# A graph layer and a recurrence on one core: states kept by step, the edge places found earlier, the first norm reordered

## The chip, the cores and the metric

One core of a Trainium2 chip. The metric is the device time of one execution in microseconds.

## The reference

```
x = x + gnn(layernorm(x))     # h = z W + b; mean over incoming edges of h[src], by dst; dst is sorted
x = x + ffn(layernorm(x))     # a recurrence over the 3125 rows, hidden state h, cell c, 256 wide each
step: i = sigmoid(xi + h V_i); g = tanh(xg + h V_c); o = sigmoid(xo + h V_o)
      c = h * c + i * g;  h = o * tanh(c)
```

x is 3125 x 256, f32, with 103,125 edges. The recurrence runs once over all rows in order; its batch is 1.

## The kernel before

**Recurrence.** The 3125 rows are cut into 125 chunks of 25 steps, which run side by side from zero, and the chunks are run again from the end of the chunk before until starts and ends agree; t counts these steps, from 1 to DONE = 70. Steps 1 to HIDDEN = 20 run inside the counting loop (`early_*`). Steps 21 to ROUGH = 28 use one product of f16 parts, later ones three. The last round is t = 46 to 70 (`LAST_ROUND` = 45). Each step is done in two halves q of 63 and 62 chunks. On DVE a half is `new_part` (L1551, ig), `cell` (L1557, c_st), and `state_next`, which waits for ACT's tanh (L863) and writes h as f16 (h16) and then as f32 in `h_states` (L1562). POOL makes the f16 rest of h (`low_part`, L618) and h times c (`old_part`, L623). PE multiplies (`full_products`, L1103): 24 products, then a wait for the rest, then 8 for the gates i and g and 4 for o. ACT has the gates (L849, L857) and the seeds of the next step in PSUM (L836, L842).

**Layout.** `h_states` lies in h_flat as (group of five steps, half of H, chunk, step in the group), so one step's columns lie five apart. Block j of 125 rows (5 chunks of 25 rows) has its x in `x_sb[:, j, :]`.

**Output.** From t = 51 on, each step ends with one block turned on PE (two transposes, `turn_out`, L1144) and added to x on DVE (`add_out`, L1614, 256 columns), after both halves; five more blocks follow at t = 70. SP stores them in six pieces of five DMAs each (L505), waits for all (L511), and then comes to `where_far` (L464), which every engine runs: it waits for a flag, loads it, and skips a general path. DVE finds that flag from the gap between starts and ends (L1653 to L1665).

**Start.** SP loads dst and the 25 parts of x (L486 to L490), ACT's queue loads w_gnn and its bias, then U, V and b of three gates (L692 to L700). DVE takes moments of the first two chunks of five blocks, then the largest and smallest of w_gnn (L1296), then scales, the deviation of chunk 0 (L1278), the low part of W, the split bias and `window_starts` (L1349), the search for the first edge of each window; POOL gathers rows (L561) and edges (L574) for it. Then the loop over blocks (L1370): ACT normalizes (L713) and rounds (L735, L740), PE transposes (L964) and multiplies (L975, L978), DVE makes the low parts (L1387, L1393), takes the moments of block j + 10 and, in the first three blocks of a chunk, the deviation of the next.

**Edges.** After that loop PE turns the window edges (L985), DVE works out from src and dst the places and keys of 625 windows of 128 edges (L1404 to L1428, with `places`, L1248), and the counting loop (L1513) begins: one-hots on DVE (L1485), counts (L1061) and sums (L989, L991) on PE, with the second norm, gates and early steps in it. PE waits for keys and for all lines before it (L1049, L1050). Two tables hand-place the rest: `weights_work` (L1470) puts the halving of the weights at window (0, 15), four reductions of U and V at (1, 0) to (2, 0), and so on. POOL's `weights_top` (L566) reduces over partitions, and `root` (L581) does the inverse roots of the second norm.

## Time and profile before

| | us |
|---|---|
| median of 3 runs | 576.62 (575.88 to 580.61) |
| profiled execution | 576.53 |
| its span, first to last instruction | 574.7 |
| outside the span | 1.83 |
| PE, DVE, ACT, POOL busy | 433.1, 406.2, 361.0, 216.2 |

A row of instructions gives the start in us from the span's start, the duration, engine and line, what is written and read, how many were merged, and in brackets the idle time before and what ended it. "PEld" is PE's weight load, "SPq" the queue on which SP issues DMAs, "issue" is time in which the engine waited for nothing that the profile shows. bank and ps tiles lie in PSUM; early tiles all carry the name gx, because they lie in it.

### The profile page before, as it was taken

Reading aid. Unit: us, or ns where it says so; the run is one execution under the profiler, and the core shown is the slowest. Engines: PE = TensorE matmul, PEld = TensorE weight load, DVE = VectorE, ACT = ScalarE, POOL = GpSimd, SP = SyncE. Lnnn points to the kernel's source line nnn. Section 1 sums busy time; section 2 is a strip of 40 time slices with the busy share of each in tenths; the row PEclk is TensorE's granted clock in tenths of the full one; section 3 lists DMA queues with packets and bytes.
Section 4 is the critical chain, followed back from the end, with each engine's and each line's share of the span. In section 5 each row is a group of like instructions: output and inputs, shape, how many; then the busy total and the mean of one; then the engine's idle time right before and its main releaser. Section 6 shows DMA issues by size and latency. Waiting matters only on the chain.

```text
span 574.7 us, 15746 instructions
## 1 busy us (share of the span) xinstructions
PE 433.1 (75%) x6225; PEld 375.2 (65%) x6225; DVE 406.2 (71%) x1124; ACT 361.0 (63%) x961; POOL 216.2 (38%) x407
## 2 busy tenths in 40 slices
PE   1008891787999899999999998754877777777760
PEld 1006670575788788888888896644766667666660
DVE  0195769978777686877788784457677777777772
ACT  0024670454556677776867775688788888777750
POOL 5104000016243253443453543312556555555530
PEclk9999996699999999999999999975899999999995
DMA  7432003300010000001000100100000000011102
GB/s 179 146 120 50 2 1 97 104 25 2 1 47 1 1 26 22 2 1 46 2 2 13 35 2 1 46 1 1 3 3 3 5 2 2 10 41 47 43 12 89
DMA packets 17319, 17.79 MB, mean 31 GB/s; under 512 B 2294, under 2 KB 16889, under 8 KB 17239
## 3 DMA queue, kind: packets, MB, share of 16 engines
q1 hardware_dynamic: 12935, 13.03, 7.0%
q10 hardware_dynamic: 2864, 1.97, 1.5%
...
q14 instruction: 28, 0.23, 0.1%
...
## 4 chain that ended last, share of the span: by engine, by line
PE 40%; DVE 32%; ACT 12%; issue 6%; SPq 3%; POOL 3%; DMA 1%; DVEq 0%; ACTq 0%
PE bank L1020 9%; PE bank L989 8%; PE bank L991 8%; DVE c_st L1557 7%; DVE ig L1551 5%; ACT tc L863 5%; DVE h L1562 5%; PE bank L978 4%; PE bank L1061 4%; SPq L490 3%; DVE h_flat L1562 3%; DVE hots L1485 3%; ACT gx L754 2%; PE bank L1103 2%; PE bank L1037 2%
## 5 line engine op out<-in xcount | busy, mean ns | idle before, releaser
L989 PE MATMUL bank<-h_flat,counts 125*128 125x257 f16 x625 | 170.9, 275 | 0.0
L991 PE MATMUL bank<-h_flat,counts 125*128 125x256 f16 x625 | 169.0, 272 | 0.0
L1103 PE MATMUL bank<-h,V 128*128 128x63 f16 (+1 forms) x3216 | 123.3, 196 | 48.2 <-DVE h L1562 45.0
L797 ACT ACTIVATE counts<-bank 125x500 f16<-125x500 f32 (+1 forms) x175 | 97.3, 557 | 95.7 <-PE bank L1061 94.2
L1103 PEld LDWEIGHTS bank<-h,V 128*128 128x128 f16 x3216 | 110.5, 99 | 62.4 <-issue 43.3
L1061 PE MATMUL bank<-hots 128*128 128x125 f16 x625 | 136.7, 226 | 17.7 <-DVE hots L1485 17.6
L1485 DVE TENSOR_TENSOR hots<-iota,kp 128x1024 f16<-128x1024 f16 x157 | 105.1, 698 | 0.1
L593 POOL TENSOR_SCALAR newton<-rstd,var_eps 125x1 f32<-125x1 f32 x50 | 42.5, 850 | 122.6 <-DVE rstd L1445 113.4
L1061 PEld LDWEIGHTS bank<-hots 128*128 128x128 f16 x625 | 60.4, 99 | 29.4 <-DVE far_f L1428 12.5
L618 POOL TENSOR_TENSOR h<-h_flat,h 128x126 f16<-128x126 f32 x82 | 42.0, 512 | 66.6 <-DVE h_flat L1562 66.6
L1020 PE MATMUL bank<-z2T,U 128*128 128x250 f16 (+1 forms) x540 | 58.5, 260 | 10.7 <-DVE z2T L1457 6.0
L989 PEld LDWEIGHTS bank<-h_flat,counts 125*128 125x128 f16 x625 | 61.7, 99 | 7.3
L991 PEld LDWEIGHTS bank<-h_flat,counts 125*128 125x128 f16 x625 | 61.6, 99 | 0.7
L1020 PEld LDWEIGHTS bank<-z2T,U 128*128 128x128 f16 x540 | 45.3, 100 | 20.1 <-issue 9.2
L1562 DVE SCALAR_TENSOR_TENSOR h<-gate,tc 128x126 f16<-128x126 f32 (+1 forms) x100 | 30.0, 300 | 31.4 <-ACT tc L863 31.1
L849 ACT ACTIVATE gate<-bank,w_unscale 128x252 f32<-128x252 f32 x100 | 46.6, 467 | 6.5 <-PE bank L1103 5.4
L863 ACT ACTIVATE tc<-c_st 128x126 f32<-128x126 f32 x100 | 30.9, 309 | 28.1 <-DVE c_st L1557 28.1
L1557 DVE SCALAR_TENSOR_TENSOR c_st<-hc,ig 128x126 f32<-128x126 f32 x100 | 44.9, 449 | 3.4
L754 ACT ACTIVATE gx<-bank,gb,gx_scale 128x250 f32<-128x250 f32 (+1 forms) x90 | 42.3, 524 | 6.1 <-PE bank L1020 6.0
L623 POOL TENSOR_TENSOR hc<-h_flat,c_st 128x126 f32<-128x126 f32 x82 | 45.8, 559 | 0.0
L964 PE MATMUL bank<-ident,gx 125*128 125x125 f32 x50 | 11.7, 326 | 37.7 <-ACT gx L713 27.0
L836 ACT ACTIVATE bank<-gx 128x252 f32<-128x252 f32 x100 | 38.4, 385 | 0.1
...
## 6 DMA issues: line engine op xcount, KB each, us to landing
...
```

Of the source, the lines that this page charges most:

```text
L754: nc.scalar.activation(gx[:, RUN * s:RUN * (s + 1), m, ROWS * k:ROWS * (k + n)], gates_bank(tile // 2)[:, half * TB * NB:half * TB * NB + ...
L797: nc.scalar.activation(counts[:, j % 2, :, n0:n0 + n], ps_count[group % 3][0:NB, 0:n * BLOCKS].rearrange("p (n s) -> p s n", n=n), ACT.Cop ...
L849: nc.scalar.activation(gate[:, q, 0:2 * HH, 0:n], ps_g[q][:, 0:2 * HH * n].rearrange("p (m k) -> p m k", k=n), ACT.Tanh, scale=w_unscale[: ...
L863: nc.scalar.activation(tc[:, q, :, 0:c1 - c0], c_st[:, c, :, c0:c1], ACT.Tanh, scale=0.5).then_inc(tc_ready[q], 1)
L989: nc.tensor.matmul(ps_sum[turn % 2][:, 0:D + 1], counts[:, turn % 2, s, :], line[:, s, D:2 * D + 1], start=(s == 0), stop=False, skip_grou ...
L991: return nc.tensor.matmul(ps_sum[turn % 2][:, 0:D], counts[:, turn % 2, s, :], line[:, s, 0:D], start=False, stop=(s == BLOCKS - 1), skip_ ...
L1020: mm = nc.tensor.matmul(gates_bank(at_unit)[:, half * TB * NB:half * TB * NB + n_blocks * NB], U16[:, w_part, d, m * P:(m + 1) * P], z2T[: ...
L1061: nc.tensor.matmul(ps_count[group % 3][:, pos * KEYS:(pos + 1) * KEYS], hots[:, ring, 0, g // 2, :, g % 2], hots[:, ring, 1, g // 2, 0:KEY ...
L1103: mm = nc.tensor.matmul(to[:, (m - m0) * n:(m - m0 + 1) * n], V16[:, v_part, d, m * P:(m + 1) * P], h16[:, h_part, d, c0:c1], start=False, ...
L1485: nc.vector.tensor_tensor(hots[:, k % RING, :, :, :, :].rearrange("p a h n g -> p (a h) n g"), iota[:, :, :].unsqueeze(1).to_broadcast(of) ...
L1557: nc.vector.scalar_tensor_tensor(out=c_st[:, c, :, c0:c1], in0=hc[:, q, :, 0:c1 - c0], scalar=0.5, in1=ig[:, q, :, 0:c1 - c0], op0=ALU.mul ...
L1562: return nc.vector.scalar_tensor_tensor(out=to, in0=gate[:, q, 2 * HH:MT, 0:n], scalar=1.0, in1=tc[:, q, :, 0:n], op0=ALU.add, op1=ALU.mult)
```

## The change

- `h_states` is ordered (step, half of H, chunk), so a step's columns are contiguous.
- x after the first layer is stored in row order (25 DMAs for 5), and read back in one DMA as `x_sb[chunk, step, :]`; DVE waits for that at t = 47. Each half q of the steps from t = 47 (48) on turns and adds 128 columns of one step (`out_parts`), on DVE between `cell` and `state_next`. At t = 70 five such pieces follow. Seven output DMAs in all, the last three with 3, 1 and 1 steps; SP waits for them behind the far test. The c part of the gap is taken before the last state, and comparison and sum of the gap become one instruction.
- Parts 3 and 4 of the first four x chunks are loaded on ACT's queue, and U, V, b on SP's behind x.
- The largest absolute value is taken in one reduction; w_gnn's stands ahead of x's moments. POOL halves the weights, and converts the window edges.
- Moments of blocks 5 to 9 come after the deviation of the first five; later ones eight blocks ahead. The window search compares and sums in one instruction (with an accumulator) and stands at j = 2.
- Places and keys are worked out on windows by edges (125 x 640) within blocks 18 to 24 of the first norm (`floors`, `edge_places`), before PE's transposes; ACT copies the result to `kp`. PE's wait for all lines moves from the loop's front to the first sum. `weights_work` moves up.

```diff
-h_states = h_flat[:, 0:STEPS * H // P * CHUNKS].rearrange("p (s m k r) -> p s m k r", s=GROUPS_S, m=HH, r=RUN)
+h_states = h_flat[:, 0:STEPS * HH * CHUNKS].rearrange("p (t m k) -> p t m k", t=STEPS, m=HH)
...
+def out_parts(t, q):
+    step = t - LAST_ROUND - (2 if q == 1 else 3)
+    parts = [(step, 1 - q)] if step >= 0 else []
+    if (t, q) == (DONE, 1):
+        parts += [(STEPS - 2, 1), (STEPS - 1, 0), (STEPS - 1, 1)]
+    return parts
+OUT_ALL = [(step, d) for step in range(STEPS) for d in range(HH)]
...
+        for r in range(3 if c < X_SHARED else RUN):
             sp.dma_start(x_sb[parts(r), js, :], x_rows[c, r, :, :, :]).then_inc(x_in[c], 16)
+    for n, (U, V, b) in enumerate(((U_i, V_i, b_i), (U_c, V_c, b_c), (U_o, V_o, b_o))):
+        sp.dma_start(U_sb[:, :, n, :], U.rearrange("(a p) h -> p a h", p=P)).then_inc(weights_in, 16)
+        sp.dma_start(V_sb[:, :, n, :], V.rearrange("(a p) h -> p a h", p=P)).then_inc(weights_in, 16)
+        with nc.allow_non_contiguous_dma("bias columns"):
+            sp.dma_start(gb[:, n, :], b.rearrange("(a p) -> p a", p=P)).then_inc(weights_in, 16)
...
+        for r in range(RUN):
+            sp.dma_start(x1_rows[s, r, :, :, :], x_sb[parts(r), s::RUN, :]).then_inc(x1_stored, 16)
+    def load_x1():
+        sp.dma_start(x_sb[:, :, :], x1_dram.rearrange("(c t) d -> c t d", t=STEPS)).then_inc(x1_back, 16)
...
+    sp.wait_ge(x1_stored, 16 * BLOCKS)
+    sp.wait_ge(z2_ready, BLOCKS)
+    load_x1()
+    def store_out(t0, t1, done):
+        sp.dma_start(out_steps[:, t0:t1, :], x_sb[:, t0:t1, :]).then_inc(done, 16)
+    pieces = [(0, 5), (5, 10), (10, 15), (15, 20), (20, 23), (23, 24), (24, 25)]
+    for t0, t1 in pieces:
+        sp.wait_ge(out_ready, HH * t1)
+        store_out(t0, t1, out_done)
+    def all_out():
+        sp.wait_ge(out_done, 16 * len(pieces))
...
+    for in_ in win_edges_in:
+        pool.wait_ge(in_, 16)
+    nc.gpsimd.tensor_copy(win_edges_f, win_edges.rearrange("p b e a -> p a b e")).then_inc(edges_f, 1)
+    weights_seq = [0]
+    def halve(w, by):
+        nc.gpsimd.tensor_scalar(w, w, by, None, ALU.mult).then_inc(halved, 1)
+        weights_seq[0] += 1
+    pool.wait_ge(weights_in, 16 * 9)
+    for n in (0, 2):
+        halve(U_sb[:, :, n, :], 0.5)
+        halve(gb[:, n, :], 0.5)
+        halve(V_sb[:, :, n, :], 0.25)
+    halve(V_sb[:, :, 1, :], 0.5)
...
+    x_rows = x.rearrange("(k i s r) d -> k r i s d", k=RUN, i=ROWS, r=RUN)
+    for c in range(X_SHARED):
+        for r in range(3, RUN):
+            act.dma_start(x_sb[r:NB:RUN, c * X_CHUNK:(c + 1) * X_CHUNK, :], x_rows[c, r, :, :, :]
+                          ).then_inc(x_in[c], 16)
...
-    for c in range(2):
-        deviation(c * X_CHUNK, (c + 1) * X_CHUNK)
+    deviation(0, X_CHUNK)
     for c in range(BLOCKS // X_CHUNK):
-        if c > 0 and (c + 2) * X_CHUNK <= BLOCKS:
-            deviation((c + 1) * X_CHUNK, (c + 2) * X_CHUNK)
+        if (c + 2) * X_CHUNK <= BLOCKS:
+            if c > 0:
+                deviation((c + 1) * X_CHUNK, (c + 2) * X_CHUNK)
         for j in range(c * X_CHUNK, (c + 1) * X_CHUNK + (2 if (c + 1) * X_CHUNK == BLOCKS else 0)):
             if j == 0:
                 act.wait_ge(scales_ready, 1)
                                      scale=w_scale[:, 0:1]).then_inc(w_hi, 1)
             if j == 0:
                 first_norm(0)
+            if j == 2:
+                deviation(X_CHUNK, 2 * X_CHUNK)
...
+    full = EDGES_FIRST * WIN_ROWS // HOT_WINDOWS
+    rest = WIN_ROWS // HOT_WINDOWS
+    for a in (PART, KEY):
+        nc.scalar.activation(kp[:, 0:full, a, :], bank[2 + a][:, 0:full * HOT_WINDOWS].rearrange(
+            "p (k g) -> p k g", g=HOT_WINDOWS), ACT.Copy).then_inc(keys_ready, 1)
+        last_ps = edges_at(a, EDGES_FIRST)
+        nc.scalar.activation(kp[:, full:full + rest, a, :], last_ps[:, 0:rest * HOT_WINDOWS].rearrange(
+            "p (k g) -> p k g", g=HOT_WINDOWS), ACT.Copy).then_inc(keys_ready, 1)
+        nc.scalar.activation(kp[:, full + rest, a, 0:1], last_ps[:, rest * HOT_WINDOWS:WIN_ROWS], ACT.Copy
...
-    pe.wait_ge(keys_ready, 1)
-    pe.wait_ge(line_ready, BLOCKS)
+    pe.wait_ge(keys_ready, 6)
...
+                    if t == 0:
+                        pe.wait_ge(line_ready, BLOCKS)
...
+        nc.tensor.transpose(ps_out[n % len(ps_out)][0:CHUNKS, 0:P], h_states[:, step, d, :], ident[:, :]
+                            ).then_inc(hT_ready, 1)
...
+    def extreme(n, w):
+        counted_op(nc.vector.tensor_reduce(w_max[:, n:n + 1], w, AX_X, ALU.max, apply_absolute_value=True))
...
+            counted_op(nc.vector.scalar_tensor_tensor(
+                out=win_rows_f[:, b, :], in0=win_rows[:, b, :], scalar=col_thr[:, b:b + 1],
+                in1=ones[0:WIN_ROWS, 0:1].to_broadcast([WIN_ROWS, EDGE_COLS]), op0=ALU.is_lt, op1=ALU.mult,
+                accum_out=in_row[:, b:b + 1]))
...
+    def floors(k):
+        if k == 0:
+            dve.wait_ge(edges_f, 1)
+        of, by = ((win_edges_f[:, 1, :, :], RUN), (edge_run, RUN), (edge_chunk, ROWS))[k]
+        floor_of((edge_run, edge_chunk, edge_k)[k], of, by)
+    def edge_places(k):
+        if k == 0:
+            link(nc.vector.scalar_tensor_tensor(out=edge_part, in0=edge_run, scalar=-float(RUN),
+                                                in1=win_edges_f[:, 1, :, :], op0=ALU.mult, op1=ALU.add))
+            link(nc.vector.scalar_tensor_tensor(out=edge_part, in0=edge_chunk, scalar=float(RUN),
+                                                in1=edge_part, op0=ALU.mult, op1=ALU.add))
+        elif k == 1:
+            nc.vector.scalar_tensor_tensor(out=edge_part, in0=edge_k, scalar=-float(RUN * ROWS), in1=edge_part,
+                                           op0=ALU.mult, op1=ALU.add).then_inc(edges_placed, 1)
+            link(nc.vector.scalar_tensor_tensor(out=edge_key, in0=edge_chunk, scalar=-float(RUN),
+                                                in1=edge_run, op0=ALU.mult, op1=ALU.add))
+        elif k == 2:
+            link(nc.vector.scalar_tensor_tensor(out=edge_key, in0=edge_k, scalar=float(RUN), in1=edge_key,
+                                                op0=ALU.mult, op1=ALU.add))
+            link(nc.vector.tensor_tensor(win_edges_f[:, 0, :, :], win_edges_f[:, 0, :, :],
+                                         col_thr.unsqueeze(2).to_broadcast([WIN_ROWS, WIN_BATCHES, WIN_EDGES]),
+                                         ALU.subtract))
+        else:
+            nc.vector.scalar_tensor_tensor(out=edge_key, in0=win_edges_f[:, 0, :, :], scalar=float(BLOCKS),
+                                           in1=edge_key, op0=ALU.mult, op1=ALU.add).then_inc(edges_placed, 1)
+    for j in range(X_CHUNK):
+        chunk_stats(j)
+    chunk_to_root(0)
     scales(0, 1, 6, 1)
     for k in range(6):
         chunk_deviation(0, k)
...
+    for j in range(X_CHUNK, 2 * X_CHUNK):
+        chunk_stats(j)
+    chunk_to_root(1)
+    AHEAD = 8
+    for j in range(BLOCKS + 4):
+        c, k = divmod(j, X_CHUNK)
+        if c + 1 < BLOCKS // X_CHUNK and 2 <= k:
+            chunk_deviation(c + 1, 2 * (k - 2))
+        if j == 1:
+            dve.wait_ge(w_hi, 1)
+            dve.wait_ge(consts, 7)
...
+        if j == 2:
+            window_starts()
...
+        if 2 * X_CHUNK <= j + AHEAD < BLOCKS:
+            chunk_stats(j + AHEAD)
+        if c + 1 < BLOCKS // X_CHUNK and 2 <= k:
+            chunk_deviation(c + 1, 2 * (k - 2) + 1)
+        if 2 * X_CHUNK <= j + AHEAD < BLOCKS and (j + AHEAD) % X_CHUNK == X_CHUNK - 1:
+            chunk_to_root((j + AHEAD) // X_CHUNK)
+        if FLOORS_FROM <= j < FLOORS_FROM + 3:
+            floors(j - FLOORS_FROM)
+        if FLOORS_FROM + 3 <= j < FLOORS_FROM + 7:
+            edge_places(j - FLOORS_FROM - 3)
+    nc.vector.memset(far_f[:, :], 0.0)
...
-    weights_work = {(0, 15): halve,
-                    (1, 0): lambda: extreme(w_max, 1, flat(U_sb), ALU.max),
-                    (1, 8): lambda: extreme(w_min, 1, flat(U_sb), ALU.min),
-                    (1, 16): lambda: extreme(w_max, 2, flat(V_sb), ALU.max),
-                    (2, 0): lambda: extreme(w_min, 2, flat(V_sb), ALU.min),
-                    (2, 4): lambda: largest(1, 3),
-                    (2, 23): lambda: scales(1, 3, 13, 2),
-                    (3, 7): lambda: x_scales(),
+    def uv_extreme(n, w):
+        if n == 1:
+            dve.wait_ge(halved, 7)
+        extreme(n, w[:, :, :, :].rearrange("p d n h -> p (d n h)"))
+    weights_work = {(0, 12): lambda: uv_extreme(1, U_sb),
+                    (0, 18): lambda: uv_extreme(2, V_sb),
+                    (0, 20): lambda: largest(1, 3),
+                    (1, 20): lambda: scales(1, 3, 13, 2),
+                    (2, 7): lambda: x_scales(),
...
+        cols = slice(d * P, (d + 1) * P)
+        nc.vector.scalar_tensor_tensor(out=x_sb[:, step, cols], in0=ps_out[n % len(ps_out)][0:CHUNKS, 0:P],
+                                       scalar=0.5, in1=x_sb[:, step, cols], op0=ALU.mult, op1=ALU.add
...
+            if t < DONE:
+                for step, d in out_parts(t, q):
+                    add_out(step, d)
+            elif q == 1:
+                for half in range(2):
+                    dve.wait_ge(c_ready[half], n)
+                counted_op(nc.vector.tensor_tensor(gap[:, 1, :, :], c_st[:, c_after(DONE), :, 0:CHUNKS - 1],
+                                                   c_st[:, C_START, :, 1:CHUNKS], ALU.subtract))
...
-    link(nc.vector.tensor_scalar(gap[:, :, :, :], gap[:, :, :, :], STATE_TOL ** 2, None, ALU.is_le))
-    nc.vector.tensor_reduce(near[:, :], gap[:, :, :, :].rearrange("p a m k -> p (a m k)"), AX_X, ALU.add
-                            ).then_inc(near_ready, 1)
+    gap_all = gap[:, :, :, :].rearrange("p a m k -> p (a m k)")
+    nc.vector.scalar_tensor_tensor(out=gap_all, in0=gap_all, scalar=STATE_TOL ** 2,
+                                   in1=ones[:, 0:1].to_broadcast([P, 2 * HH * (CHUNKS - 1)]), op0=ALU.is_le,
+                                   op1=ALU.mult, accum_out=near[:, :]).then_inc(near_ready, 1)
```

## Rows read from the trace of the kernel before

**Rows 1.** Busy time by stretch, one of them, its granted clock and DMA.

```profile
core 0: us, PE busy (x) PEld busy (x) DVE busy (x) ACT busy (x) POOL busy (x), PEclk, DMA share, GB/s
...
126.00:380.00 254.00, 236.63 (x2531) 208.51 (x2531) 183.91 (x455) 173.25 (x375) 104.96 (x190) 0.99 0.04 14
```

**Rows 2.** Chain that ended last, the start: start us, us, what.

```profile
28.23 1.73 DVE stats L1269 x5
...
39.63 2.38 DVE gx L1356
```

**Rows 3.** DMA queue 1, 12:16 us, then 28:32 us: packets, MB, share.

```profile
q1 hardware_dynamic: 163, 0.16, 14.4%
...
q1 hardware_dynamic: 490, 0.48, 34.1%
```

**Rows 4.** Chain that ended last, the first norm on PE.

```profile
47.01 1.47 PE bank L978 x6
...
49.30 1.49 PE bank L978 x6
...
67.38 0.80 PE bank L978 x6
...
68.64 0.81 PE bank L978 x6
...
85.55 1.08 PE bank L985 x10
```

**Rows 5.** Instructions in order, DVE, 91 to 99 us: start, us, what, [idle before].

```profile
91.98 0.49 DVE L1240 TENSOR_SCALAR gx<-gx 128x625 f32<-128x625 f32 x1
...
93.03 3.34 DVE L1255 SCALAR_TENSOR_TENSOR gx<-gx 128x625 f32<-128x625 f32 x4
...
98.12 0.69 DVE L1485 TENSOR_TENSOR hots<-iota,kp 128x1024 f16<-128x1024 f16 x1
```

**Rows 6.** Instructions in order, ACT at 99.6 us, POOL at 123 us.

```profile
99.62 2.27 ACT L797 ACTIVATE counts<-bank 125x500 f16<-125x500 f32 x4 [13.65 <-PE bank L1061]
...
123.07 0.33 POOL L593 TENSOR_SCALAR newton<-rstd,var_eps 125x1 f32<-125x1 f32 x1 [6.76 <-issue]
```

**Rows 7.** Instructions in order, all engines, full steps without output.

```profile
463.63 0.28 DVE L1562 SCALAR_TENSOR_TENSOR h_start<-gate,tc 128x122 f32<-128x122 f32 x1
...
466.64 0.29 DVE L1562 SCALAR_TENSOR_TENSOR h<-gate,tc 128x124 f16<-128x124 f32 x1 [0.37 <-ACT tc L863]
...
466.85 0.38 DVE L1562 SCALAR_TENSOR_TENSOR h_flat<-gate,tc 128x124 f32<-128x124 f32 x1
...
467.07 1.34 PE L1103 MATMUL bank<-h,V 128*128 128x62 f16 x36 [0.36 <-DVE h L1562]
...
467.20 0.29 DVE L1551 SCALAR_TENSOR_TENSOR ig<-gate 128x126 f32<-128x126 f32 x1
...
467.53 0.46 DVE L1557 SCALAR_TENSOR_TENSOR c_st<-hc,ig 128x126 f32<-128x126 f32 x1
...
468.34 0.47 ACT L849 ACTIVATE gate<-bank,w_unscale 128x248 f32<-128x248 f32 x1
...
468.36 0.29 DVE L1562 SCALAR_TENSOR_TENSOR h<-gate,tc 128x126 f16<-128x126 f32 x1 [0.38 <-ACT tc L863]
```

**Rows 8.** Instructions in order, all engines, full steps with output.

```profile
549.95 0.42 DVE L1614 SCALAR_TENSOR_TENSOR x_sb<-bank,x_sb 125x256 f32<-125x256 f32 x1
...
550.29 0.55 DVE L1551 SCALAR_TENSOR_TENSOR ig<-gate 128x126 f32<-128x126 f32 x1
...
551.11 0.46 PE L1144 MATMUL bank<-ident,h_flat 128*125 128x128 f32 x2
...
552.14 1.21 PEld L1103 LDWEIGHTS bank<-h,V 128*128 128x128 f16 x36 [0.76 <-issue]
```

**Rows 9.** The end in order of time; then SP's waits: us, times, longest.

```profile
557.00 0.29 DVE L1562 SCALAR_TENSOR_TENSOR h<-gate,tc 128x124 f16<-128x124 f32 x1 [0.37 <-ACT tc L863]
...
557.86 12.34 SPq L505 DMA_DIRECT2D out_dram<-x_sb  x15
...
SPq L467 <- DMA out_dram<-x_sb: 2.8, 1, 2.8
```

250 lines of the change are left out of this document (80 added, 170 removed).

## The prediction, made before the result was known

> **What bounds the kernel now.** I read the table of stages first, then the chain of waits at both ends, then single instructions. The table [rows 1] is to show that no one engine bounds everything. In the middle (126 to 380 us) PE works 236.6 of 254 us, and the change leaves that loop's work as it is; I take it at no gain. The other stages are bound by order and by waits:
>
> - Until 43.6 us PE does almost nothing. The chain [rows 2] runs over the arrival of x (the second chunk's moments start at 28.23), two reductions over w_gnn, the split of its weights, then the window search: five comparisons (1.83) and, at 39.63, a reduction of 2.38. Only at 43.68 does PE go on. While x loads its queue moved 0.16 MB in four us, later 0.48 MB [rows 3].
> - From 43.7 to 85.5 PE is the chain: 2.29 us a block at first, 1.26 us from 59.4 on [rows 4] (47.01 to 49.30; 67.38 to 68.64). The granted clock stands at 1.00 in both stretches, yet the same six matmuls take 1.47 and 0.80 us, which is the ratio of 1.2 and 2.4 GHz. 25 blocks so would be 38.7, and the stretch takes 41.9: at three chunk borders ACT waits for the next chunk's moments, and PE behind it.
> - From 85.5 to 98.1 only DVE works: the edge places, nine passes of 0.48 and four of 0.82 among them [rows 5]. Then come the one-hots with seven halvings and four reductions between them, and PE's sums after 8.6 us more.
> - The steps t = 21 to 28 take 2.9 us, not touched. Full steps t = 29 to 50 take 3.43 us, t = 51 to 70, which also turn and add an output block, 3.87 us [rows 7, 8].
> - After the last state (557.0) SP issues 15 output DMAs in 12.3 us, then waits 2.8 us for the last and goes through the far test [rows 9].
>
> **Start.** In the changed kernel w_gnn's reduction (one, with absolute value) runs before x is there. The 1.54 MB of U and V follow x instead of going beside it; that is 0.1 us of edit on SP's queue (nine issues, each under 1 us, behind the last x issue) and is hidden by x's transfer. x itself arrives sooner: 1.28 MB (two chunks) and 0.21 MB of dst at 120 GB/s [rows 3] are 12.4 us, so 14.3 us from the first packet at 1.9 is one bound; the other is today's 28.2. Between them lie w_gnn with its bias (0.38 MB), the window rows (1.07 MB), and two further chunks' parts that ACT's queue brings forward: I count about 2.2 MB at the same 120 GB/s and take 21 us. From there: five moments and their sums 2.3, weight split 0.75 and bias 1.7 as now, five scalar_tensor_tensor over 425 columns (0.16 fixed plus 0.66 x 425/625 from the 0.82 row of [rows 5], so 0.6 each, 3.0) and four small ones 0.7: 29.5, and PE at about 30.3, against 43.68. Chance for this to be off by 3 either way. Gain 13.4.
>
> The use of a second queue for two fifths of x is where a rule weighs. The row: with one queue at work, and 125 partitions, the engines' mean busy share is 0.34 at 120 GB/s [rows 3]. The Trainium skill, DMA: Bandwidth & Descriptors, section on why a DMA increments its semaphore by 16, says that a DMA uses the largest number of engines up to 16 that divides its slowest dimensions, which gives 5 of 16 for 125 or 25 rows, and the same lowest ones for both queues. The trace agrees (5/16 = 0.31). By it the second queue adds no bandwidth and brings only order; without it chunk 1 could be there at 15 and the sum would be 6 us lower.
>
> **First norm.** 7 blocks of 2.29 and 18 of 1.26 are 38.7; the moments are eight blocks ahead, so the first stall hides on the slow clock. At the two later borders ACT still waits at the head of block 10 and 15 for moments that DVE ends one block later by its own count, about 1.2 us each (a line's low part, five short sums, 0.2 for the variance): 2.4. And DVE now does the edge work inside it: 9 passes of 0.48 and 8 of 0.83 (640 columns, from [rows 5]) are 11 us in seven blocks. Its other work there is 0.66 a block of 1.26 [rows 4], so 15.2 us stand against 8.9: plus 6.3. PE ends at 30.3 + 38.7 + 2.4 + 6.3 = 77.7 instead of 85.55. If the clock comes up sooner, the bound is 7 x 1.03 = 7 us less; if DVE delays fully, 2 more. The window edges come in 12 us earlier than now with their search, so POOL's five gathers (7.5 us) and its conversion are done by about 46 and wanted at about 60. POOL's seven halvings (DVE, at 512 columns, would need no more each than the 0.48 of [rows 5]; three times that is 10 us in all) wait for weights at about 42 and are wanted at 80: hidden, with the roots queued behind them wanted at 95.
>
> **From the last line to the one-hots.** Now 12.6 us (85.55 to 98.12 [rows 4, 5]). Then: ten transposes 1.1, six copies on ACT, 500 columns in 0.56 [rows 6] and shorter, together 1.9, and 0.15 of hand-over: 3.2. Gain 9.4. So the one-hots start at 80.9, 17.2 us earlier than now.
>
> **Counting.** The halvings and two reductions leave, but PE is bound by its sums from window 28 on, and up to there DVE goes from 8.6 to 8.3: 0.3. PE also waits 1.46 us at 126.1 for a root that POOL began 3.7 us after its guess was ready [rows 6]; the reduction over partitions before it moves a block up, which I expect to free that. 1.8 in all (0 to 4).
>
> **Steps.** A half-step [rows 7] is a ring on DVE: h16 at 466.64, h_flat 0.21 later, ig 0.35 later, c 0.33, and h16 again 0.83 after c (c 0.46, tanh, 0.03); 1.72 in all. The state is now written with a stride of five; with contiguous columns the h_start row gives 0.28 for 0.38, and the next instruction comes 0.20 after it instead of 0.35. That alone would be 1.57. But there is a second ring: h16 to PE 0.43, 32 matmuls to the gate 1.26, gate and hand-over 0.50, ig to c 0.33, c to h16 0.83, in all 3.35 for two half-steps, so 1.67 each. I take 0.05 a half-step, 0.1 a step, 2.2 us over 22 steps (bounds 0, if POOL's subtraction then collides with ig, and 6.6 at 1.57).
>
> In t = 51 to 70 the 0.42 of the addition stands after h_flat and pushes ig into POOL's subtraction, where it takes 0.55 instead of 0.29 [rows 8]. The change puts an addition of 128 columns (0.16 fixed and half of the rest: 0.29) between c and h16, where DVE is idle 0.37 for the tanh: it starts about 0.42 after c and ends by 0.71, before 0.83. PE has one transpose (0.23, half of 0.46 [rows 8]) before it would be idle 0.36. So the steps go to 3.34: 20 x 0.53 = 10.6. Behind the waiting addition stands h16 and behind it everything, so if it isn't hidden it costs its 0.29 per half-step, 48 times 0.29 = 14, and the gain is gone. The new steps 47 to 50 are hidden alike. Before them DVE waits for x1 read back: 3.2 MB at 120 GB/s are 27 us from about 370 of today's time, wanted at 470. The 25 stores of x1 for 5 cost SP 0.75 each in 51 us gaps.
>
> **End.** Counted from today's last state: five additions of 0.29 end at 558.7 instead of 560.6. The last three pieces are three DMAs instead of 15, the last issued by 560.0. The transfer is late next: 0.64 MB at about 115 GB/s from 559.1 is 5.6, plus 0.4: 565.1, and 0.3 to the end. The far test (three passes of 0.55 to 0.7, then 0.8, then 1.7 as in 573.0 to 574.7 [rows 9]) is over at 563.3 and now runs beside it. 565.4 for 574.7: gain 9.3 (8 to 11).
>
> **The sum.** 13.4 - 5.5 (the first norm, 47.4 for 41.9) + 9.4 + 1.8 + 2.2 + 10.6 + 9.3 = 41.2. The profiled execution took 576.53, of which 1.83 lie outside the span and stay: 535.3, say 535. The median of the runs is 576.62, the same.
>
> **Rivals.**
> 1. x comes no sooner (28.2): PE starts at 37.5, 7.2 less gained: 542. For it: the gathers of the window rows stay where they are, and they too hold x back. Against it: x gets three times the rate once the others are through [rows 3]. 0.12.
> 2. The additions aren't hidden, or ig and the sums collide with POOL as at 550.29 [rows 8]: steps t = 51 to 70 stay at 3.87: 546. 0.12.
> 3. The first norm runs on the fast clock early, or the edge work fits: 7 less, 528. Nothing in [rows 4] speaks for it: PE was as busy then as now. 0.12.
> 4. Slower: the transposes after each half of a step. If each of them breaks PE's stream and pays its 0.46 and the 0.76 of idle weight loading that [rows 8] show before a block of products, a half-step is 1.34 + 0.46 + 0.76 = 2.56 instead of 1.93. That is 25 us over 20 steps and 7 over steps 47 to 50, with the step gains of 12.8 gone: 535 + 13 + 32 = 580. It decides only if a half-step is above 2.5 us; today's transposes end 0.6 before the next products. 0.02.
> 5. A part doesn't do what it says (the stall of POOL or of a chunk border stays, the last transfer is slower): 541 to 545. 0.07.
> The forecast itself, 529 to 541: 0.55.
>
> **Range and chances.** 523 to 549 takes in rivals 1 to 3 and 5 and the bounds of x, clock and steps; sums of several misses lie outside. A measurement tells 1% (5.8 us) from no change. All cases but rival 4 lie over 5% below: faster 0.96, same 0.02, slower 0.02.
>
> **What would show it.** First norm: PE's steady start near 30 us and at chunk borders gaps of 1.2 us at most; DVE dense with 0.48 and 0.83 passes near the end; one-hots at 81 or so. Steps: h_flat at 0.29, h16 to h16 1.67 us, the additions between c and h16, ACT's tanh unmoved. End: three output issues after the last state, the span's end 8 us behind it instead of 17.7. Wrong, if x's second chunk comes after 25, if the half-step with additions is over 1.75, or if the last DMA takes over 8 us.

## The result, and the profile after

| | before | after |
|---|---|---|
| median, us | 576.25 (575.75 to 580.61, 4 runs) | 545.45 (542.79 to 548.26, 4 runs) |
| profiled execution | 576.53 | 545.82 |
| its span | 574.7 | 544.0 |

The ratio of the runs is 0.945, 95% interval 0.9384 to 0.9517: faster. The forecast was 535.0 with the range 523 to 549, so the time lies in the range but 10 us above the forecast, and outside the 529 to 541 given for the likeliest case. Two single runs reported or used below were in a slower state (547.19 of experiment 8, whose median without it is 542.64, and one of the kernel before beside experiments 5 to 8), and every ratio leaves them out. The span lost 30.7 us where the sum said 41.2. By stage, from the two traces:

| stage | forecast | measured | how measured |
|---|---|---|---|
| PE goes on with the first norm | 13.4 | 10.0 | 43.68, now 33.68 |
| first norm | -5.5 | -5.4 | 41.9 [rows 4], now 47.3 (33.68 to 80.94) |
| last line to one-hots | 9.4 | 9.8 | 12.57 [rows 5], now 2.73 |
| counting, gates, t up to 28 | 1.8 | 2.0 | the first full step's ig at 404.73, now 388.29 |
| t = 29 to 50 | 2.2 | 1.2 | 76.22, now 75.06 |
| t = 51 to 70 | 10.6 | 7.5 | 76.05, now 68.53, to the last h16 |
| behind the last h16 | 9.3 | 5.6 | 17.7, now 12.1 |

Of 10.5 us missed, 3.4 lie at the start, 4.1 in the steps and 3.7 at the end; the other stages give 0.7 back.

**Start.** The kernel after, instructions in order on POOL, DVE and PE (start, us, what, idle before and its releaser):

```profile
9.21 1.54 POOL L582 DMA_INDIRECT gx<-in_dst_dram,gx  x1 [4.49 <-DVE gx L1311]
16.84 0.38 POOL L577 PARTITION_ALL_REDUCE w_top<-w_max  x1 [6.09 <-issue]
17.44 1.43 POOL L582 DMA_INDIRECT gx<-in_dst_dram,gx  x1 [0.23 <-issue]
...
22.21 1.21 POOL L582 DMA_INDIRECT gx<-in_dst_dram,gx  x1 [0.30 <-issue]
...
9.74 0.15 DVE L1307 TENSOR_SCALAR w_max<-w_max 128x1 f32<-128x1 f32 x1
...
21.16 1.73 DVE L1321 BATCH_NORM_STATS2 stats<-x_sb 125x6 f32<-125x256 f32 x5 [2.40 <-DMA x_sb<-in_x_dram]
...
29.60 0.66 DVE L1378 SCALAR_TENSOR_TENSOR gx<-gx,ones 125x425 f32<-125x425 int32 x1 [3.56 <-DMA gx<-in_dst_dram,gx]
...
33.68 0.65 PE L1010 MATMUL bank<-ident,gx 125*128 125x125 f32 x2 [13.06 <-DVE gx L1444]
```

x did what was forecast: its second chunk is there at 21.16 (forecast 21) instead of 28.23 [rows 2]. What is late next is the window rows, for which DVE waits until 29.6: w_max was known at 9.9, yet POOL stood still for 6.1 us before the reduction, with four of the five gathers behind it.

**First norm.** Busy time by stretch of the kernel after (length, PE, PEld, DVE, ACT, POOL, granted clock, DMA share, GB/s):

```profile
34.00:44.00 10.00, 9.65 (x40) 6.95 (x39) 5.61 (x24) 4.48 (x13) 5.58 (x5) 1.00 1.03 225
44.00:53.00 9.00, 7.72 (x55) 5.78 (x54) 7.83 (x32) 6.71 (x20) 1.36 (x1) 1.00 0.17 41
53.00:57.00 4.00, 4.00 (x19) 3.25 (x18) 3.04 (x10) 2.21 (x7) 1.30 (x1) 0.58 0.00 0
57.00:70.00 13.00, 9.12 (x61) 6.43 (x60) 11.30 (x36) 8.69 (x24) 6.45 (x7) 1.00 0.00 0
70.00:77.00 7.00, 6.92 (x27) 4.86 (x27) 6.83 (x13) 2.86 (x8) 0.00 (x0) 0.51 0.00 0
```

Its instructions in order, ACT and PE at a chunk border:

```profile
59.74 0.21 ACT L740 ACTIVATE sd<-var_eps 125x5 f32<-125x5 f32 x1 [1.37 <-DVE var_eps L1275]
...
60.49 0.44 PE L1010 MATMUL bank<-ident,gx 125*128 125x125 f32 x2 [1.28 <-ACT gx L746]
```

And its chain that ended last, from the last line to the one-hots:

```profile
80.94 1.08 PE bank L1031 x10
...
83.67 2.50 DVE hots L1522 x4
```

The column to read is the granted clock. The six matmuls of a block take 1.54 or 0.87 us. The first four blocks are slow and from 43.93 they are fast. The 1.00 that the column prints for these four, and that [rows 4] were read with, is no measurement: the trace's record of the clock begins at 42.7 (in the kernel before at 59.3, where its blocks turn fast), and where there is no record the view prints 1.00. These blocks take the same 1.54 us as later ones at a recorded 0.50. The grant falls to 0.50, the level of 1.2 GHz, from 53.0 to 56.4 and from 70.05 to 76.9, and five more blocks take 1.4 to 1.54. PE had been busy 7.7 of 9 us before the first fall and 9.1 of 13 before the second. In the kernel before the record has 1.00 from 59.3 to 90.0, though PE was as busy there (8.8 of 10 us from 64 to 74, 11.0 of 11 from 74 to 85). By block starts on PE the 24 intervals are 24 x 1.26 = 30.2, plus 8.6 for slow blocks, 3.0 at two chunk borders and 3.7 where PE waits for DVE's edge work.

These are numbers of one trace. Experiments 3 to 8 and 11 leave the code up to the one-hots as it is, and their traces start the one-hots at 83.2 to 87.5 us (83.67 here), with 7 to 11 slow blocks (nine here). So a difference of less than 4 us in this stage between two single traces can be the clock alone. Part of it comes back later: experiments 3, 4, 7, 8 and 11, which change nothing before the first full step, reach it at 387.1 to 389.0 (388.29 here).

**Steps.** The kernel after, instructions in order, a step with output:

```profile
504.98 0.43 POOL L652 TENSOR_TENSOR h<-h_flat,h 128x124 f16<-128x124 f32 x1 [0.63 <-DVE h_flat L1599]
505.04 0.51 DVE L1588 SCALAR_TENSOR_TENSOR ig<-gate 128x126 f32<-128x126 f32 x1
...
505.93 0.28 DVE L1652 SCALAR_TENSOR_TENSOR x_sb<-bank,x_sb 125x128 f32<-125x128 f32 x1
506.04 0.31 ACT L909 ACTIVATE tc<-c_st 128x126 f32<-128x126 f32 x1 [0.37 <-DVE c_st L1594]
...
506.39 0.29 DVE L1599 SCALAR_TENSOR_TENSOR h<-gate,tc 128x126 f16<-128x126 f32 x1 [0.18 <-ACT tc L909]
```

The same view, one of the few steps in which both begin together, without output:

```profile
442.40 0.55 POOL L652 TENSOR_TENSOR h<-h_flat,h 128x124 f16<-128x124 f32 x1 [0.67 <-DVE h_flat L1599]
442.40 0.29 DVE L1588 SCALAR_TENSOR_TENSOR ig<-gate 128x126 f32<-128x126 f32 x1
```

The addition stands in DVE's idle time before h16, of which 0.18 is left: hidden, as forecast. But ig of the first half begins 0.06 behind POOL's subtraction and takes 0.51, in the steps without output too. Where the two begin together, ig takes 0.29 and POOL 0.55. From ig to ig a step is 3.40 to 3.50 us in the first case (up to 3.87 at the ends of rounds) and 3.28 in the second (419 to 442 us only).

**End.** The kernel after, instructions in order:

```profile
531.88 0.28 DVE L1599 SCALAR_TENSOR_TENSOR h<-gate,tc 128x124 f16<-128x124 f32 x1
...
532.59 1.28 SPq L519 DMA_DIRECT2D out_dram<-x_sb  x3
...
535.97 0.14 DVE L1712 CAST far_i<-far_f 1x1 int32<-1x1 f32 x1
```

Its busy time by stretch, columns as above:

```profile
538.00:540.00 2.00, 0.00 (x0) 0.00 (x0) 0.00 (x0) 0.00 (x0) 0.00 (x0) 0.50 0.36 120
540.00:542.00 2.00, 0.00 (x0) 0.00 (x0) 0.00 (x0) 0.00 (x0) 0.00 (x0) 0.50 0.04 12
```

And SP's waits (us in total, times, longest):

```profile
SPq L74 <- DMA out_dram<-x_sb: 3.3, 1, 3.3
SPq L74 <- PEq L74: 2.3, 1, 2.3
```

Three issues end at 533.9 and the data flow until about 540.2, 7.6 us behind the first issue and 8.3 behind the last state. From there to the end of the span pass 3.8 us, 2.3 of them SP's wait for PE's queue.

### The profile page after: what moved, and what is told of

It reads as the page before. It is cut to its first block, busy times and chain, and to the rows that moved or that the text cites. A ratio compares the mean times of both kernels' runs of the same rounds, so it can differ in the third digit from the quotient of the medians.

```text
span 544.0 us, 15807 instructions
## 1 busy us (share of the span) xinstructions
PE 429.0 (79%) x6225; PEld 372.5 (68%) x6225; DVE 389.8 (72%) x1135; ACT 361.2 (66%) x967; POOL 217.3 (40%) x415
## 4 chain that ended last, share of the span: by engine, by line
PE 48%; DVE 23%; ACT 14%; issue 7%; POOL 5%; DMA 2%; DVEq 0%; ACTq 0%; POOLq 0%
PE bank L1066 9%; PE bank L1035 9%; PE bank L1150 9%; PE bank L1037 9%; PE bank L1106 5%; DVE ig L1588 4%; DVE c_st L1594 4%; ACT gate L895 4%; DVE h L1599 3%; ACT tc L909 3%; ACT gx L789 3%; PE bank L1024 2%; PE bank L1083 2%; DVE hots L1522 2%; POOL newton L627 2%
## 5 line engine op out<-in xcount | busy, mean ns | idle before, releaser
L1150 PE MATMUL bank<-h,V 128*128 128x63 f16 (+1 forms) x3216 | 115.5, 195 | 44.3 <-DVE h L1599 39.1
L1150 PEld LDWEIGHTS bank<-h,V 128*128 128x128 f16 x3216 | 106.7, 99 | 56.3 <-issue 41.4
L627 POOL TENSOR_SCALAR newton<-rstd,var_eps 125x1 f32<-125x1 f32 x50 | 43.7, 874 | 126.0 <-DVE rstd L1480 123.5
L652 POOL TENSOR_TENSOR h<-h_flat,h 128x126 f16<-128x126 f32 x82 | 36.5, 446 | 70.3 <-DVE h_flat L1599 70.3
L1588 DVE SCALAR_TENSOR_TENSOR ig<-gate 128x126 f32<-128x126 f32 x100 | 35.4, 354 | 12.8 <-ACT gate L895 9.3
L1594 DVE SCALAR_TENSOR_TENSOR c_st<-hc,ig 128x126 f32<-128x126 f32 x100 | 37.1, 371 | 3.4
L657 POOL TENSOR_TENSOR hc<-h_flat,c_st 128x126 f32<-128x126 f32 x82 | 38.5, 470 | 0.0
```

Source lines behind the costliest of these rows:

```text
L627: link(nc.gpsimd.tensor_scalar(t, y, v, y, ALU.mult, ALU.mult))
L1150: mm = nc.tensor.matmul(to[:, (m - m0) * n:(m - m0 + 1) * n], V16[:, v_part, d, m * P:(m + 1) * P], h16[:, h_part, d, c0:c1], start=False, ...
L1588: nc.vector.scalar_tensor_tensor(out=ig[:, q, :, 0:n], in0=gate[:, q, 0:HH, 0:n], scalar=1.0, in1=gate[:, q, HH:2 * HH, 0:n], op0=ALU.add, ...
L1594: nc.vector.scalar_tensor_tensor(out=c_st[:, c, :, c0:c1], in0=hc[:, q, :, 0:c1 - c0], scalar=0.5, in1=ig[:, q, :, 0:c1 - c0], op0=ALU.mul ...
```

## The experiments

Each is an edit of the changed kernel. "Last state" is the last h16 write, "steps" the time from the first full step's ig to it: 143.6 in the changed kernel, 152.3 in the one before. Traces of unchanged code differ by up to 4.3 us in a stage, as said above, so for the steps and the end the profile decides, not the median. By the intervals of the ratios alone only experiments 4, 9, 10 and 12 are told apart from the changed kernel (0.9384 to 0.9517).

**1. The reduction behind the gathers.**

```
-                if b == 0:
-                    weights_top(1, 0, 1)
+            weights_top(1, 0, 1)
```

> The changed kernel, with the reduction over w_gnn's maxima (L577) put behind all five gathers of the window rows, as in the kernel before, instead of behind the first. In the changed kernel POOL stands still for 6.0 us (10.84 to 16.84, called issue) between the first gather and the reduction, though w_max was ready at 9.9; the last window row lands at about 29.5 and PE goes on at 33.68. Theory: those 6 us are POOL's own, something it must do before its first reduction, and they begin when POOL comes to that instruction. Then the gathers run from 9.2 to 16.7, the last rows land at about 23.7, the reduction runs at about 22.7 instead of 16.84, the weight split and bias end at about 27, the window search of 3.5 follows, and PE goes on at about 31: 2 to 3 us less in all, 543. Rival A: the 6 us are a wait for the first gather or for w_max; then the reduction starts at once behind the last gather, at 16.9, and PE goes on at about 28: 6 us less. Rival B: the rows land when x lets them, not when POOL issues them: they land at 29.5 as now and PE stays at 33.7: no change, 545.5.

545.39 us (544.2 to 546.31), ratio to before 0.9464 (0.9412 to 0.9516). POOL's instructions in order:

```profile
15.60 1.20 POOL L582 DMA_INDIRECT gx<-in_dst_dram,gx  x1 [0.30 <-issue]
23.20 0.38 POOL L577 PARTITION_ALL_REDUCE w_top<-w_max  x1 [6.40 <-issue]
```

The stall moves along with the reduction (6.4 us, all gathers over): it is POOL's own, and rival A falls. Rival B falls too: the last packet of the rows ends at 22.8 instead of 28.9, and the search waits for rows no more; it begins at 29.84, right behind the bias. But now the scale is late, so the second chunk's moments move to 25.03 and the split bias ends at 29.8, and PE goes on at 33.87. My 31 missed that DVE's order puts those moments behind the scale.

**2. The reduction ahead of the gathers.**

```
+            weights_top(1, 0, 1)
             pool.wait_ge(rows_known, 1)
...
-                if b == 0:
-                    weights_top(1, 0, 1)
```

> The changed kernel, with the same reduction ahead of all gathers and ahead of POOL's wait for the row numbers. POOL is then idle from 4.72 to the reduction. Theory (the 6 us are POOL's own and can pass while it would wait anyway): they run from 4.8 to 10.8, the reduction stands at about 10.9, the five gathers from 11.5 to 18.8 instead of 9.2 to 23.4, the last rows land at about 25 to 26, and PE goes on at about 29 to 30 instead of 33.68: 4 us less, 541.5. Rival A (the 6 us wait for w_max or for a gather): the reduction comes at about 10 (w_max) and the same follows half a us earlier, or 6 us of idle appear elsewhere, behind the reduction. Rival B (the rows land when x lets them): they land at 29.5 as now, no change, 545.5.

545.52 us (542.86 to 549.39), ratio 0.9469 (0.9398 to 0.954). Instructions in order, POOL and PE:

```profile
12.56 0.38 POOL L577 PARTITION_ALL_REDUCE w_top<-w_max  x1 [7.85 <-issue]
...
31.57 0.65 PE L1008 MATMUL bank<-ident,gx 125*128 125x125 f32 x2 [12.99 <-DVE gx L1442]
```

POOL is idle for 7.85 us here, but that is not the stall's length: w_max was ready only at 11.13, 1.4 us before the reduction, so part of it may be that wait. The search begins at 27.5 and PE goes on 2.1 us earlier. Yet the one-hots start at 84.28, 0.6 later than in the changed kernel: the grant is 0.79 in 44 to 54 and 0.70 in 54 to 64, where the changed kernel has 0.95 and 0.88, and ten blocks are slow instead of nine. In this trace the earlier start was paid back in clock; whether the one causes the other isn't shown, since 84.28 lies within the 83.2 to 87.5 of unchanged code. (At the second reduction, over U and V, the changed kernel has POOL idle from 63.5 to 90.9, and no root is held up; in the kernel before its root stood 6.76 us behind the reduction [rows 6]. The same gap of "issue", 6.86 us, now stands before POOL's first halving at 55.70, where nothing waits for it.)

**3. POOL's subtraction waits for the gates.**

```
                 old_part(0, h_before(t), c_before(t))
+                pool.wait_ge(ig_gate[0], n)
                 low_part(1, h_before(t), n - 1)
                 old_part(1, h_before(t), c_before(t))
                 if t < DONE:
+                    pool.wait_ge(ig_gate[1], n)
                     low_part(0, h_after(t), n)
```

> The changed kernel; POOL waits, before each subtraction of the state's low part (L652), for the same gates that DVE's ig of the other half waits for. In the changed kernel the full steps stand mostly in a mode of 3.43 us in which L652 begins 0.07 to 0.09 before ig of the first half and ig takes 0.46 to 0.52; for some steps near 440 us L652 and ig begin together, ig takes 0.29 and L652 0.53, and a step is 3.25. Theory: of DVE and POOL on two operations that meet, the one that starts later is held up, and what sets the step is ig. Then ig takes 0.29 in both halves, L652 0.5, a step 3.25 to 3.3, and over the 42 full steps 6 to 7.5 us go: 538.5. Rival A: the low products on PE then come late, since the subtraction ends 0.1 to 0.2 later than they want it: the step stays at 3.43 or grows to 3.5: 545 to 549. Rival B: who is held up isn't set by who begins first: ig still takes 0.5, 545.5.

542.27 us (540.65 to 548.39), ratio 0.9444 (0.9366 to 0.9521). The profiled span is 538.8, and the steps take 139.6 for 143.6. Instructions in order, DVE and POOL, a step with output:

```profile
501.35 0.29 DVE L1590 SCALAR_TENSOR_TENSOR ig<-gate 128x126 f32<-128x126 f32 x1
501.40 0.52 POOL L652 TENSOR_TENSOR h<-h_flat,h 128x124 f16<-128x124 f32 x1 [0.68 <-DVE h_flat L1601]
```

Nearly every step is 3.28 us now, with output or without, and ig takes 0.29 in both halves; the subtraction's 0.52 is early enough for PE. The order is turned by 0.11 us (POOL 0.06 ahead, now 0.05 behind), and that is all it takes. The theory's 6 to 7.5 was 4.0 in this trace: seven steps had been at 3.28 before, and some, mostly at the ends of rounds, keep 3.4 to 3.9. The Trainium skill, SBUF — State Buffer, section on the two separate sides, says that VectorE, in an operation with two inputs in SBUF, and GpSimd, in one that reads SBUF, share one pair of ports as a lock which the one that starts first holds for its whole instruction, while the other is blocked. The trace agrees on who is held up (ig 0.51 behind POOL and 0.29 ahead of it; POOL 0.52 behind ig and 0.43 ahead). It does not bear out the whole instruction: ig ends 0.14 us behind the end of POOL's subtraction, and POOL 0.28 behind the end of ig, where each would need its own 0.29 and 0.43.

**4. The additions behind the state.**

```
-                    if t < DONE:
-                        for step, d in out_parts(t, q):
-                            add_out(step, d)
...
                     state_next(q, t)
+                    if t < DONE:
+                        for step, d in out_parts(t, q):
+                            add_out(step, d)
```

> The changed kernel, with each output addition of 128 columns placed behind the two writes of the state (as in the kernel before) instead of ahead of them, where DVE waits for the tanh. The layout of the states stays. Theory: in the changed kernel the addition lies in DVE's idle time before the h16 write (0.17 of 0.37 left), and is free; behind the state it stands on the chain to ig in every half-step and pushes ig into POOL's subtraction: 0.28 per half-step plus up to 0.2, so steps t = 47 to 70 take 4.0 to 4.4 us instead of 3.47, 24 steps: 13 to 22 us more, 559 to 567. Rival: ig waits for the gates of ACT anyway (0.17 idle in the first half), and the small addition is hidden there in one half: 3.7 a step, 5.5 us more, 551.

552.83 us (551.36 to 554.69), ratio 0.9583 (0.9531 to 0.9636). DVE's instructions in order:

```profile
504.69 0.28 DVE L1652 SCALAR_TENSOR_TENSOR x_sb<-bank,x_sb 125x128 f32<-125x128 f32 x1
504.90 0.52 DVE L1588 SCALAR_TENSOR_TENSOR ig<-gate 128x124 f32<-128x124 f32 x1
```

Steps 51 to 70 take 76.39 us, as before the change (76.05), for 68.53. So without the new place of the additions nothing of the gain of these steps is left. Its size lies between theory and rival: 3.82 to 3.93 a step where 4.0 to 4.4 and 3.7 were said. Both halves now have ig at 0.51 to 0.54; what takes up the rest of the 0.28 per half wasn't tested.

**5 and 6. The old layout of the states, alone and with the wait of experiment 3.**

```
-h_states = h_flat[...].rearrange("p (t m k) -> p t m k", ...)
+h_runs = h_flat[...].rearrange("p (s m k r) -> p s m k r", ...)
```

> The changed kernel with the old layout of the states in h_flat (a stride of five between columns), all else as changed: additions between c and h16, transposes by halves, output by steps. In the kernel before the full steps without outputs take 3.43 us with ig at 0.29 in both halves; in the changed kernel 3.43 too with ig at 0.46 to 0.51 in one half, and 3.28 in the few steps in which ig is 0.29 in both. Theory: the contiguous layout shortened DVE's ring from 1.72, but all of it went to the collision of ig with POOL's subtraction, so the old layout costs next to nothing: 3.43 to 3.45 us a step throughout, ig at 0.29, from the first full step to the last state 145 to 146 us instead of 143.6: 547. Rival: the layout carries part of the gain with outputs, since the wider 0.38 write beside the addition pushes ig: 3.6 to 3.7 us a step there, 550 to 552.

> The kernel with the old, strided layout of the states and, besides, POOL's wait for the gates (as in the run that gave 3.28 us a step with the contiguous layout). Theory: with the strided layout DVE's own ring of 1.72 us a half-step sets the pace (h16, h_flat, ig, c, tanh), so the wait has nothing to gain: 3.43 to 3.47 a step, 547, and the two edits are worth something only together. Rival: the ring was itself made of POOL's share, and the wait brings it to 3.3: 541 as with the contiguous layout.

547.65 (545.53 to 548.42), ratio 0.9518 (0.9448 to 0.9587), and 546.89 (545.15 to 552.49), ratio 0.9504 (0.9437 to 0.957). Steps: 144.5 and 146.5 for 143.6. In the first nearly every step is at 3.42 to 3.46 with ig at 0.29 in both halves, and steps 51 to 70 take 68.32: the layout gave nothing there. In steps 29 to 50 it gave 1.1 (76.19, now 75.06). With the wait the strided kernel is no better (3.44 to 3.49 a step, and 2.0 us more over all steps, in a trace that is the slowest of its five runs), while the contiguous one falls to 3.28. So the layout shortened DVE's ring, and the collision took nearly all of it: alone the layout gave 0.9 us over all steps, layout and wait together 4.9.

**7. The last pieces cut otherwise.**

```
-(20, 23), (23, 24), (24, 25)]
+(20, 22), (22, 24), (24, 25)]
```

> The changed kernel with its last three output pieces cut as (20, 22), (22, 24), (24, 25) instead of (20, 23), (23, 24), (24, 25). In the changed kernel the addition for step 22's second half comes only after the last state (532.3), so 625 KB (pieces of 375, 125 and 125) go out from 533.2 to 540.2, at about 100 GB/s, and the span ends at 544.0, 12.1 behind the last state's 531.88. Theory: the transfer alone sets the end; with 375 KB left the last packets land 2.3 to 2.5 us earlier, and the end is 9.6 behind the last state: 543. Rival: the tail is held by what follows the transfer and by the fixed part of a DMA (the far test on SP, the last wait of 2.3): less than 0.5 us gained, 545.5.

543.74 us (541.0 to 544.86), ratio 0.9444 (0.9374 to 0.9514); 10.5 us behind the last state for 12.1. The transfer ends 6.15 us behind the last state instead of 8.3, but SP's wait for PE's queue grows from 2.3 to 3.8: a second bound stands 1.6 us below the first.

**8. The output on more DMA engines.**

```
-                sp.dma_start(out_steps[:, t0:t1, :], x_sb[:, t0:t1, :]).then_inc(done, 16)
+                for c0, c1 in ((0, 112), (112, CHUNKS)):
+                    sp.dma_start(out_steps[c0:c1, t0:t1, :], x_sb[c0:c1, t0:t1, :]).then_inc(done, 16)
```

> The changed kernel with each output piece issued as two DMAs, chunks 0 to 111 and 112 to 124, instead of one over 125 chunks. The output transfer shows a mean busy share of 0.30 to 0.33 of 16 DMA engines at about 100 to 115 GB/s. Theory: each DMA is spread over as many DMA engines as divide its outer dimension (at most 16), so 125 gives 5, 112 gives 16 and 13 gives 13; then the share is over 0.8, the last 625 KB take 2.5 to 3.5 us instead of 7, less a longer issue on SP (0.5 to 0.7 more per DMA, three more behind the last state), and the end is about 8.5 to 9.5 us behind the last state instead of 12.1: 542.5. The Trainium skill, DMA: Bandwidth & Descriptors, section on why a DMA increments its semaphore by 16, states that rule; by it the same. Rival: the transfer is bound by something other than the number of engines (one issue at a time, or the memory): share and rate stay where they are, and with six issues for three the end comes 1 us later: 546.5.

543.56 us (538.57 to 547.19), ratio 0.9422 (0.9313 to 0.9531). SP's waits at the end:

```profile
SPq L74 <- PEq L74: 4.4, 1, 4.4
SPq L467 <- DVE far_i L1713: 0.9, 1, 0.9
```

In 532 to 534 us the mean busy share is 0.85 at 259 GB/s, where the changed kernel has 0.36 at 120 GB/s at best (538 to 540). The rule of the Trainium skill (DMA: Bandwidth & Descriptors, why a DMA increments its semaphore by 16) holds: the trace agrees. The 625 KB are out before the far test is through, and SP waits for no output any more. What is left is 10.24 us behind the last state, where 8.5 to 9.5 were expected: 4.2 to the far test's flag and 6.0 from its flag (534.8) to the end. In these 6 us no engine is busy, the queues fetch instructions (0.09 MB in 536 to 541) and SP waits for PE's queue.

**9. The edge work behind the first norm.**

```
-            FLOORS_FROM = 18
+            FLOORS_FROM = BLOCKS + 4
...
+            for k in range(3):
+                floors(k)
+            for k in range(4):
+                edge_places(k)
```

> The changed kernel with the whole edge work of DVE (three floors, four parts of places and keys: 17 passes of 0.49 to 0.83) behind the last block of the first norm, instead of inside blocks 18 to 24. In the changed kernel, by the starts of its blocks on PE, 25 blocks are 24 x 1.26 plus 8.6 on a slower clock, 3.0 at the chunk borders and 3.7 where PE waits for DVE in the last blocks. Theory: without edge work PE ends the first norm 3.7 earlier (77 instead of 80.9), then 11 us of passes lie bare, and the one-hots start at about 91 instead of 83.7: 7 us more in all, 552.5. Rival A: DVE doesn't hold PE at all there and the slow clock sets the last blocks: PE ends at 80.9, the one-hots start at 94.5: 556. Rival B: without DVE's holes PE runs denser and its clock falls sooner or for longer (1.54 us for six matmuls instead of 0.87): PE ends within 1.5 us of 80.9, with more blocks at 1.54 than the changed kernel's nine: 555.

550.53 us (549.54 to 552.91), ratio 0.9566 (0.9534 to 0.9598). PE's last block starts at 74.86 instead of 80.08, and 10.5 us of bare passes bring the one-hots to 91.18. So inside the norm the edge work costs PE 5.2 us and outside 10.5 and more. Seven blocks are slow, not nine, so part of the 5.2 is clock; where PE waits for DVE it was 3.7. Against the 83.2 to 87.5 of unchanged code the loss at the one-hots is 3.7 to 8.0, not a firm 7.5.

**10. The weights' loads beside x again.**

```
-    X_SHARED = 4
+    X_SHARED = 0
```

And the nine loads of U, V and b move from SP's queue, behind x, to ACT's, behind w_gnn.

> The changed kernel with the loads as before: all of x on SP's queue, and U, V and b on ACT's queue right behind w_gnn, so that they go beside x. Theory: x's bytes share five DMA engines with the 1.5 MB of weights; the first chunk's moments start at about 20.5 instead of 13.0 and the second's at about 28 instead of 21.2; the weight split, bias and window search follow, PE goes on at about 36.5 instead of 33.7: 2.8 more, 548. Rival A: the weights fill DMA engines that x does not use (x keeps to five), so x is hardly later: second chunk at 22 to 23, no change, 545.5. Rival B: PE's start is later, but a later start gives a faster clock in the first norm (in the run with the reduction first, PE went on 2.1 earlier and ended the first norm 0.6 later, at a lower granted clock): one-hots within 1 us of 83.7, 545.5.

551.67 us (550.62 to 556.12), ratio 0.9599 (0.9558 to 0.964). Busy time in 6 to 14 and 14 to 18 us, columns as above:

```profile
6.00:14.00 8.00, 2.23 (x10) 2.17 (x10) 1.46 (x5) 1.28 (x1) 1.53 (x1) 1.00 0.95 230
14.00:18.00 4.00, 0.00 (x0) 0.00 (x0) 0.00 (x0) 0.00 (x0) 1.19 (x2) 1.00 0.33 117
```

The second chunk's moments start at 28.10, as said, and the first blocks' products 3.3 us later. The DMA engines are busy to 0.95 in 6 to 14 us, where most of the weights come. In 14 to 18 us three queues share 0.33 and 117 GB/s: x has 0.12 of the engines, the rest of the weights 0.07 and the first window rows 0.14, so x does not have even this third to itself. The two edits together, order and queue of the loads, are thus worth 7 us of arrival; which of them it is wasn't separated. The one-hots come 6.0 us later, not 3: ten slow blocks instead of nine, and stalls behind later chunks (2.1 us later than the latest of unchanged code). Rival B, that the clock gives it back, falls here.

**11. The wait for the gates and the split output**, the edits of experiments 3 and 8 together.

> The changed kernel with both edits that gained: POOL's subtraction waits for the gates, and each output piece goes out as two DMAs (112 and 13 chunks). Theory: they touch different stages and add up: 5.2 us less in the steps (143.6 to 138.6 from the first full step to the last state) and 1.9 less behind the last state (10.2 for 12.1): 7 us below 545.5, 538.5. Rival: with the steps shorter the output additions or the transposes come late, and the gain in the steps is under 4 us: 541.

540.0 us (538.87 to 544.03, 6 runs), ratio 0.9389 (0.9358 to 0.942), span 537.6. Steps 139.64, and 10.4 behind the last state: they add up (4.0 and 1.7). The 5.2 expected of the steps was too much, as experiment 3 had given 4.0.

**12. The same, and the moments nine blocks ahead.**

```
-            AHEAD = 8
+            AHEAD = 9
```

> The kernel with the gate wait and the split output, and in the first norm the moments of x nine blocks ahead instead of eight. In the changed kernel the deviation of a chunk on ACT waits 1.37 us for var_eps (59.74), and PE 1.28 behind it, at each of the borders before blocks 10, 15 (block starts 2.77 apart instead of 1.26). Theory: the last moments of a chunk now stand one block earlier on DVE, the variance is there when ACT comes to it, and the two or three stalls shrink from 1.5 to at most 0.3: PE ends the first norm about 2.5 us earlier (78 instead of 80.5), 537.5. Rival: PE is denser and its granted clock falls to 0.50 sooner or for longer; with one or two more blocks at 2.29 the gain is gone: one-hots within 1 us of 83.3, 540.

534.43 us (532.35 to 536.62, 6 runs), ratio 0.9257 (0.9223 to 0.9292): the fastest kernel here, 11.0 us below the changed one. Busy time by stretch:

```profile
34.00:64.00 30.00, 26.60 (x162) 19.79 (x162) 25.78 (x95) 20.98 (x57) 15.03 (x13) 1.00 0.36 86
...
65.00:71.50 6.50, 6.50 (x26) 4.52 (x25) 6.29 (x13) 2.66 (x7) 0.00 (x0) 0.50 0.00 0
```

The border stalls fell from 1.5 and 1.8 to 1.0 and 0.2, and the grant stays at 1.00 until 65: six slow blocks where experiment 11 had seven. PE ends the norm 2.8 us earlier, and the one-hots start at 80.5, outside the 83.2 to 87.5 of unchanged code. The first gates come 4.85 earlier (123.54 for 128.39); the grant was higher in the counting too (1.00 for 0.88 in 94 to 104), and how much of the rest is its doing isn't shown. The rival, denser work and a worse clock, was wrong here. In experiment 2 the clock was worse. What decides between them stays open.

## Why the prediction was right or wrong

- **x sooner: right.** 21.16 for a forecast of 21, and experiment 10 shows that it is the loads' new order and queues. As the rule of the Trainium skill that was weighed there had it (DMA: Bandwidth & Descriptors, why a DMA increments its semaphore by 16), the second queue brought no bandwidth: 0.35 of the DMA engines at 117 GB/s from 6 to 14 us.
- **PE's start: wrong by 3.4.** The step that failed is "five moments and their sums 2.3, weight split 0.75 and bias 1.7 as now, five scalar_tensor_tensor ...: 29.5". It has no term for the window rows. I took them as there, since in the kernel before they were; but the reduction now stands among their gathers, and brings 6.1 us of POOL's own. In the kernel before that stall lay in 16 us of waiting, and [rows 6] showed its like (6.76, called issue), which I read as freed by a move and not as a cost that travels with the reduction. Experiments 1 and 2 show that it travels. By experiment 2 PE could go on 2.1 us sooner, but neither order brought the one-hots forward by more than 0.3: another operand or the clock is late next.
- **First norm: the total right (47.3 for 47.4), the parts not.** "7 blocks of 2.29" were nine, four at the start and five in two later falls of the granted clock; borders 3.0 for 2.4; edge work 3.7 of waiting for "plus 6.3". The errors cancelled, and the hit to 0.1 is luck: unchanged code gives 7 to 11 slow blocks. The prediction's own sum was off too (seven blocks of 0.66 and 11 us are 15.6, not 15.2), and so were its premises on the clock: the 1.00 at the slow blocks was no record, and 1.47 to 0.80 us is a ratio of 1.84, not of 2.
- **One-hots: right** (2.7 for 3.2). **Counting: 2.0 for 1.8**, which proves little: from one-hots to first full step the kernels that leave this stage alone take 301.6 to 304.6 us, for 306.6 before. Its parts weren't tested.
- **Steps 29 to 50: the case of the lower bound came true.** "Bounds 0, if POOL's subtraction then collides with ig" is what happened in most steps. The term was 2.2 and measured 1.2, nearly all of it in the seven steps at 3.28.
- **Steps 51 to 70: mechanism right, size off.** The addition is hidden, and experiment 4 shows that nothing of the gain is left without its new place. "So the steps go to 3.34" failed: they went to 3.40 to 3.50, as ig still meets the subtraction. Rival 2 took the collision as the end of all gain; it costs 0.2 in one half. Experiment 3 gives 3.28, so the forecast of PE's ring (1.67 a half-step) was 0.03 too high, once nothing else is in the way.
- **End: wrong by 3.7.** The step that failed is "and 0.3 to the end". The transfer itself ended when it was said to: 565.1 is 8.1 us behind the last state, and its data end 8.3 behind it (slower than said, but begun earlier). What comes behind it took 3.8 instead of 0.3. The other branch was mis-sized too: "The far test ... is over at 563.3", 6.3 behind the last state, with a last 1.7 us to the end of the span; experiment 8, which has no transfer left to wait for, shows 10.2, with 6.0 from the flag to the end. [Rows 9] could not show it, being covered by the 12.3 us of issues.
- **"Wrong if":** x's second chunk came before 25, the half-step with output is 1.73 on average, and the last DMA stayed under 8 us; none of the three signs came. Of the signs for being right, h16 to h16 at 1.67 and the end 8 us behind the last state were missed (1.73 and 12.1). Rival 4 (transposes break PE's stream) did not occur. Rival 5 comes nearest to the 545: three parts fell short, each by 3 to 4 us. A stall of POOL is among them, though at w_gnn's reduction and not before the roots; the last transfer, which it also named, is not.
